# Block transposes on VectorE that read two elements apart in place of four, and write two apart in place of 64

## The reference, cut to what matters

```python
# x: (8, 32, 64, 64) float32; stage 0: per-pixel 3x3 filter with softmax weights
x = _L0_conv_ref(x, w1, b1, w2, b2)
for j in range(4):
    Kj = project(K[j]); Lj = project(L[j])
    z = conv3x3(x, Kj)                          # conv1
    z = relu(batchnorm(z, gamma[j], beta[j]))
    z = conv3x3T(z, Kj)                         # conv2
    x = x + 0.1 * z
    x = batchnorm(x, gamma[j], beta[j])
    x = diag_imp_conv_fft(x, Lj, 0.1)           # ifft2(fft2(x) / (0.1 * |fft2(Lj)|^2 + 1))
```

## Time and profile before

| | us |
|---|---|
| median of 3 runs | 746.18 (745.37 to 751.39) |
| profiled execution, its own time | 744.98 |
| span of the profile | 742.9 |
| busy: TensorE matmul | 663.8 (89%) |
| busy: VectorE | 562.4 (76%) |
| busy: ScalarE | 264.7 (36%) |
| share of the chain that ended last | TensorE 53%, VectorE 35%, ScalarE 5% |

### The profile page before, as it was taken

The page is one execution under the profiler, slowest core; times in us unless marked ns, Lnnn a source line. Parts: engine busy times, 40 slices in busy tenths (PEclk is TensorE's granted clock), DMA queues, the critical chain, the costliest instruction groups (busy, mean ns, idle before and its releaser), DMA issues.

```text
span 742.9 us, 13258 instructions
## 1 busy us (share of the span) xinstructions
PE 663.8 (89%) x5408; PEld 223.9 (30%) x5408; DVE 562.4 (76%) x875; ACT 264.7 (36%) x416; POOL 95.5 (13%) x92
## 2 busy tenths in 40 slices
PE   7689999999879979998999899988997999899982
PEld 3223333222223333222233332222333322223330
DVE  3578778874997895549988945499789554998883
ACT  1465666643900032439000324390003243900033
POOL 0376666760000000000000000000000000000000
PEclk9698999999998999999899999999899999989997
DMA  9992111119200022771000228700002287000034
GB/s 182 181 172 57 31 30 30 30 38 221 69 1 1 1 58 59 182 159 44 1 1 1 65 51 198 154 35 1 1 1 58 58 184 159 4 1 1 1 85 143
DMA packets 44638, 51.05 MB, mean 69 GB/s; under 512 B 36386, under 2 KB 36515, under 8 KB 42531
## 3 DMA queue, kind: packets, MB, share of 16 engines
q1 hardware_dynamic: 40098, 48.92, 30.5%
q10 hardware_dynamic: 4480, 1.30, 1.1%
HBM read 11.92 MB, written 4.19 MB: 22 GB/s over the span
## 4 chain that ended last, share of the span: by engine, by line
PE 53%; DVE 35%; ACT 5%; issue 3%; DMA 1%; SPq 1%; POOL 0%; DVEq 0%; ACTq 0%; POOLq 0%
PE psum L936 30%; PE psum L1010 6%; DVE work L837 6%; PE psum L1073 4%; DVE X L827 4%; DVE stats L830 4%; DVE tabT L821 3%; DVE work L881 3%; DVE work L853 3%; DVE work L847 2%; PE psum L1120 2%; PE psum L959 2%; PE psum L1106 2%; ACT Z L567 2%; DVE spare L853 2%
## 5 line engine op out<-in xcount | busy, mean ns | idle before, releaser
L936 PE MATMUL psum<-Z,wts 128*32 128x512 f32 x1536 | 171.9, 603 | 6.6 <-DVE Z L809 6.4
L936 PE MATMUL psum<-X,wts 128*32 128x512 f32 x1536 | 170.1, 593 | 0.2 <-DMA X<-X 0.2
L741 DVE BATCH_NORM_STATS2 stats<-Z 128x6 f32<-128x512 f32 x60 | 41.2, 692 | 74.7 <-ACT Z L504 74.6
L936 PEld LDWEIGHTS psum<-Z,wts 128*32 128x32 f32 x1536 | 51.3, 111 | 129.1 <-issue 116.1
L582 ACT ACTIVATE work<-psum 128x64 f32<-128x64 f32 x16 | 4.4, 277 | 219.6 <-PE psum L1097 219.6
L567 ACT ACTIVATE Z<-Z,small 128x512 f32<-128x512 f32 (+4 forms) x92 | 79.9, 922 | 5.2 <-DVE small L799 4.7
L936 PEld LDWEIGHTS psum<-X,wts 128*32 128x32 f32 x1536 | 47.6, 109 | 111.5 <-issue 110.2
L504 ACT ACTIVATE Z<-psum 128x512 f32<-128x512 f32 x64 | 38.1, 595 | 104.0 <-PE psum L936 92.7
L1106 PE MATMUL psum<-work,cstS 128*128 128x512 f32 x128 | 59.2, 605 | 4.7 <-DVE work L847 3.9
L1073 PE MATMUL psum<-work,cstS 32*64 32x512 f32 x384 | 38.4, 716 | 21.2 <-DVE work L881 9.9
L1089 PE MATMUL psum<-work,cstS 128*128 128x496 f32 x128 | 56.2, 582 | 0.0
(11 more groups left out here) (114 smaller groups left out, 805.7 us busy)
## 6 DMA issues: line engine op xcount, KB each, us to landing
X<-X SPq DMA_DIRECT2D x64, 260.0 KB, 3.9
Z<-Z SPq DMA_DIRECT2D x32, 520.0 KB, 8.1
Z<-x SPq DMA_DIRECT2D x36, 128.0 KB, 4.2
out<-Z SPq DMA_DIRECT2D x24, 128.0 KB, 2.3
parS<-par SPq DMA_DIRECT2D x4, 673.0 KB, 8.2
Z<-x SPq DMA_DIRECT2D x12, 120.0 KB, 5.0
Z<-x ACTq DMA_DIRECT2D x14, 64.0 KB, 4.2
Z<-x SPq DMA_DIRECT2D x14, 64.0 KB, 4.9
```

Of the source, the lines that this page charges most:

```text
L936: last = nc.tensor.matmul(out_b[C * r:C * r + C, :], weights[:, o:o + C], rows(src, reg, bp, g, CH, dj - 1), start=(dj == 0), stop=(dj == ...
```

## The change

`turn` is called for odd chunks only and turns the two chunks c - 1 and c with two transposes of 512 elements, one for each image: each reads the pixels of one image, which lie two elements apart in X0, and writes runs of 32 in order. A chunk's own transpose read four elements apart before. The pixels that land on one partition group are other ones, so the table of forward_w is reordered to fit (`constants`), and forward_w waits for half as many counts. `move_slots` writes its bank into one block of 512 of `backw`, two elements apart, in place of over the whole tile, 64 apart. inverse_w then picks its columns from `backw` in runs of 16, and `move_back` reads its banks 16 elements apart to put them back in order.

```diff
@@ -831,11 +831,13 @@
 
             def turn(c):
 
-                bp, q = divmod(c, Q)
-                o = bp * REG + CH * q * GROUP
-                src = X0[:, o + 2:o + 2 + CH * GROUP].rearrange("p (g i) -> p g i", i=GROUP)[:, :, 0:ROW]
-                nc.vector.transpose(turned[c // 2 % 3][:, N * (c % 2):N * (c % 2) + N],
-                                    src.rearrange("p g (l x) -> p g x l", x=4)).then_inc(rows_turned, 1)
+                k, g = c // 2, 2 * CH
+                o = c // Q * REG + CH * (c % Q - 1) * GROUP
+                src = X0[:, o + 2:o + 2 + g * GROUP].rearrange("p (g i) -> p g i", i=GROUP)[:, :, 0:ROW]
+                for b in range(2):
+                    dst = turned[k % 3].rearrange("p (m b c) -> p b m c", b=2, c=C)
+                    last = nc.vector.transpose(dst[:, b], src.rearrange("p g (e l b) -> p b g e l", e=2, b=2)[:, b])
+                last.then_inc(rows_turned, 1)
 
             def move_rows(j, c):
 
@@ -849,7 +851,7 @@
             def move_slots(j, c):
                 n, (bp, q) = NUMBER["invH", j, c], divmod(c, Q)
                 bk.full(n)
-                dst = backw[bp % 2][:, :].rearrange("p (h b c) -> p c b h", b=2, c=C)[:, 8 * q:8 * q + 8]
+                dst = backw[bp % 2][:, N * q:N * q + N].rearrange("p (c h b) -> p c b h", b=2, c=8)
                 nc.vector.transpose(dst, bank(n)).then_inc(drained[n % BANKS], 1)
 
             def move_back(j, bp, half):
@@ -861,7 +863,7 @@
                 if k > 2:
                     dve.wait_ge(x_back, NCH * j + 2 * (k - 2))
                 nc.vector.transpose(turned[k % 3].rearrange("p (m e l) -> p e m l", e=2, l=32),
-                                    psum[:, b0:b0 + 2, :].rearrange("p e n -> p (e n)")).then_inc(rows_back, 1)
+                                    psum[:, b0:b0 + 2, :].rearrange("p e (c m) -> p e m c", c=C)).then_inc(rows_back, 1)
 
             def scale_slot0(j, bp):
                 n = NUMBER["slot0", j, bp]
@@ -896,7 +898,8 @@
                             link(ins)
                             aggregate()
                     elif what == "turn":
-                        turn(at[1])
+                        if at[1] % 2:
+                            turn(at[1])
                     elif what == "fwdW":
                         move_rows(*at)
                         if at[1] == 3 * Q + 3 and j + 1 < DEPTH:
@@ -1062,7 +1065,7 @@
             def forward_w(j, bp):
 
                 first = NUMBER["fwdW", j, bp * Q]
-                pe.wait_ge(rows_turned, NCH * j + Q * bp + Q)
+                pe.wait_ge(rows_turned, PAIRS * j + 2 * bp + 2)
                 for r in range(R):
                     bk.claim(first + r)
                 for hi in range(2):
@@ -1118,7 +1121,8 @@
                         for half in range(2):
                             k, n = slice(64 * half, 64 * half + 64), first + 2 * half + hi
                             last = nc.tensor.matmul(bank(n)[C * r:C * r + C, :], cstS[k, C_IW + 32 * hi:C_IW + 32 * hi + 32],
-                                                    backw[bp % 2][k, N * r:N * r + N], start=True, stop=True,
+                                                    backw[bp % 2][k].rearrange("p (c r m) -> p r c m", c=C, r=R)[:, r],
+                                                    start=True, stop=True,
                                                     tile_position=(64 * half, C * r))
                             if r == R - 1:
                                 last.then_inc(filled[n % BANKS], 1)
@@ -1160,7 +1164,7 @@
 
     fw = np.stack([cos, -sin], 1)
     fw[:, 1, 0] = alternating
-    c[:, C_FW:C_FW + 128] = np.tile(fw.reshape(32, 128), (R, 1))
+    c[:, C_FW:C_FW + 128] = np.tile(fw.reshape(2, 32, 64).transpose(1, 0, 2).reshape(32, 128), (R, 1))
 
     iw = np.stack([2 * cos, -2 * sin], 1)
     iw[:, 0, 0], iw[:, 1, 0] = 1 / 8, alternating
```

## The result

The changed kernel takes 717.34 us (median of 4 runs, 717.11 to 718.69), before 745.77 us: a ratio of 0.9615, 95% interval 0.9588 to 0.9642. Its profiled execution took 717.11 us, with a span of 715.3 us in place of 742.9.

A forecast was written before the change was run, and what follows sets the result against it. VectorE was taken to pace conv2's first stretch, TensorE nearly the next and all of conv1; 17.3 + 5.0 + 2.4 + 3.6 + 0.4 = 28.7 us off 744.98 gave 716.3, stated as 717 us; range from 709 to past 732 us.

The forecast's parts named there:

- The price: Each 512-element `turn` and `move_slots` on VectorE falls from 1119 and 1037 ns to 681 ns, as `move_rows`.
- the ScalarE bound: Both transposes cost about 755 ns, from ScalarE's 73 ns extra for writing two apart; total 721 us.
- half the price: Rival: about 900 ns a `turn` and 860 a `move_slots` remain, total 732 us; chance 0.12.
- Stretch A: First add of conv2 to forward_w of batch pair 1, VectorE bound: ten faster turns per layer save 17.3 us in all.
- The clock: First and third layers: forward_w of pair 1 and four conv2 chunks behind it leave 1.2 GHz, saving 5.0 us.
- the end of B: Before forward_w of pair 2: TensorE's 0.61 us wait for VectorE goes in four layers, 2.4 us.
- a slow stretch in another forward_w: Sign of being wrong: the 1.2 GHz stretch moves to another forward_w that TensorE's path contains.
- The end of C: Before forward_w of pair 3: of TensorE's 1.83 us wait, 0.9 us goes in each of four layers, 3.6 us.
- The tail: Last layer, before the last inverse_h: about half of TensorE's 0.78 us wait for ScalarE goes, 0.4 us.
- Nothing elsewhere: inverse_w's runs of 16, `move_back`'s PSUM reads 16 apart, weights and semaphore counts were taken to cost nothing.
- The hand-over behind C: From forward_w of pair 3 to conv1, TensorE and VectorE hand over with unchanged steps; the 0.9 us arrive at conv1.
- the 0.7 us that I had added to the sum: The sum gave 716.3 us; with the runs' median 1.2 us above the profiled execution, 717 us was forecast.

The follow-up runs named there:

- the stride kernel: A separate kernel of only 512-element VectorE block transposes and ScalarE copies at various distances: reads two apart 671 ns, four apart 1045 ns.
- The turns alone: The kernel before with only the new `turn`, its count and its table; `move_slots`, inverse_w and `move_back` as before: 723.26 us, ratio 0.9714.
- the way back alone: The kernel before with only the new `move_slots`, inverse_w and `move_back`; `turn` as before: 737.24 us, ratio 0.9897.
- one transpose per chunk: The changed kernel with both images in one 512-element transpose, run with its own chunk, still reading two apart: 715.55 us, ratio 0.9584.
- work put into the wait: The changed kernel with forward_w of pair 1 one chunk later: 711.51 us; also with a single transpose per chunk and banks put back: 707.59 us.

## Why the prediction was right, point by point

717 us were forecast, 717.34 measured. The terms hold up unequally.

- *The price.* 681 ns taken, 684 and 674 to 696 measured; the ScalarE bound (755 ns) and half the price fall, by the stride kernel above too.
- *Stretch A*, 17.3 us: 17.04. VectorE stayed last, as worked out: TensorE still waits 0.46 us (1.13 in the first layer, where under 1 us was forecast) ahead of slot_0_back. The turns alone bring 16.7 us of it, the way back alone none.
- *The clock*, 5.0 us, and *the end of B*, 2.4 us: together 4.53 in place of 7.4. The clock is the term that was mis-sized. The first and third layers gave both (22.9 to 19.69 us), and the wait at the end of B is gone in all four, some 2.8 us. But in the second and fourth forward_w of pair 1, which TensorE's path contains, now ran at 1.2 GHz: 21.34 - 19.69 = 1.65 us lost in each. So the clock gave some 1.7 us in place of 5.0. Before, those layers had their 1.2 GHz stretch inside A, hidden by VectorE. I had taken waits of 1.34 us to be harmless, as they left no slow forward_w before. The prediction named a slow stretch in another forward_w among what would make it wrong.
- *The end of C*, 3.6 us: 3.81.
- *The tail*, 0.4 us: 0.05. TensorE's wait for ScalarE stayed (0.77 us, before 0.78). The step that failed is that pair 2's `move_slots` makes ScalarE late: the `move_back` behind it starts 10.58 us after forward_w of pair 3 in both profiles (706.65 to 717.23, 679.10 to 689.68). VectorE now is ready for it 1.14 us early and waits for inverse_w:

```profile
689.68 1.25 DVE L865 STREAM_TRANSPOSE third<-psum 128x1024 f32<-128x1024 f32 x1 [1.14 <-PE psum L1123]
```

- *Nothing elsewhere*: inverse_w is unchanged (594 and 595 ns a matmul), `move_back` too (1224 and 1229 ns, before 1223 and 1209). The hand-over behind C gained 0.2 to 0.4 us per layer that I had not counted.
- That the sum came out at 717 has luck in it: what B and the tail fell short by, 3.2 us, is nearly made up by 1.28 us that the first stage was shorter in this execution, 0.89 us behind C, and the 0.7 us that I had added to the sum. The mechanism of A, C and the price is no luck; that the clock's miss was covered is.

Open: what decides in which layer TensorE's clock falls. Waits of about 0.5 and 1.34 us stand ahead of forward_w of pair 1 in the second to fourth layers of the changed kernel, of the turn alone and of one transpose per chunk. It ran slow in two of these layers, in none and in one. So the length of these waits alone doesn't tell. Nor does VectorE's pace in A: the turn alone has the same short A and no slow forward_w, while the way back alone has the long A, with 1.27 us and more ahead of slot_0_back, and a slow forward_w of pair 1 in all four layers. With work put into the wait none of eight layers ran slow; as the turn alone has none either, with the waits, that speaks for the cure but doesn't prove it.

## What to carry to other kernels

Look at a slow VectorE instruction's access pattern in bytes: where each access fell on other 16 bytes than the one before it, 512 elements took 1.0 to 1.1 us in place of 0.67, and a layout in which two accesses in a row fall on the same 16 bytes, not necessarily a contiguous one, was as good as in order. When an engine that paces a stretch is sped up, work out what the other engine needs for the same stretch, and give what stands alone at the stretch's end its own term: there the place of an instruction counts as much as its price. Where TensorE's clock falls is a risk of its own: a new schedule can put a slow stretch on the path, so give it a term with a range, and look for it in every layer of the profile.

## What the runs showed of the hardware that was not expected

The old price doesn't grow with distance at all: reads 16 apart take 1002 ns, 8 apart 1057, 4 apart 1045, all below the 1119 ns of the old `turn`. ScalarE pays alike for reads: 614 ns in order, 646 ns two apart and 1102 ns four apart. And the layers in which forward_w of pair 1 fell to 1.2 GHz were the same in two profiles of one kernel, but others in kernels with the same waits.
